# A four-layer network in fourteen stages: the semaphores of a stage are cleared together, mostly in front of the next stage's work on GpSimd

## The reference, cut to what matters

```python
xn = _layernorm(x, axis=-1)
s = _L0_attn_ref(xn, ...)          # layer 0: an RWKV-like recurrence over time
g = _silu(_L0_ffn_ref(xn, ...))    # layer 0: 48 experts, each takes the tokens that score highest
x = x + s * g
...                                # layers 1 to 3 in the same form
return x
```

## The kernel before, in words

| Stage function | Rounds behind it | Semaphores cleared |
|---|---|---|
| `open_phase` | 4 | 26 |
| `rwkv_pre_phase` | 3 | 101 (4, 1, 96) |
| `scan_and_experts_phase` | 6 | 156 (1, 108, 8, 17, 6, 16) |
| `rwkv_close_phase` | 4 | 32 |
| `split_and_choose_phase` | 6 | 50 |
| `attention_and_experts_phase` | 7 | 71 |
| `close_and_split_phase` | 4 | 42 |
| `maxima_and_mlp_phase` | 9 | 50 |
| `causal_phase` | 3 | 20 |
| `inertia_phase` | 1 | 22 |
| `norm_and_split_phase` | 3 | 30 |
| `column_attention_phase` | 3 | 14 |
| `l2_gelu_and_rows_phase` | 2 | 24 |
| `ssm_phase` | 3 | 86 (52, 2, 32) |
| together | 58 | 724 |

## Time and profile before

### The profile page before, as it was taken

One profiled execution on the slowest core, in us unless ns is written; L12 is line 12 of the kernel. 1 busy time (PEld: TensorE's weight loads), 2 busy tenths in 40 slices (PEclk: granted clock), 3 DMA queues, 4 the chain that ended last, 5 costly groups with the idle time before them and its releaser, 6 DMA issues. The chain is left out here.

```text
span 3016.3 us, 37549 instructions
## 1 busy us (share of the span) xinstructions
PE 2424.1 (80%) x10280; PEld 1059.8 (35%) x10280; DVE 2173.8 (72%) x5978; ACT 1702.1 (56%) x3085; POOL 1015.0 (34%) x979
## 2 busy tenths in 40 slices
PE   6665477885869989769999989967778888868887
PEld 2211266662334434333333333323331111224443
DVE  6999589994676665455555646668659999667776
ACT  4454344543646666441211248855569999777775
POOL 0222589981334544140000024400020000038886
PEclk8777567767879999889999999989889999989999
DMA  3112676415456655331011113300031111011110
GB/s 127 56 56 70 154 134 110 89 25 141 136 154 136 118 114 110 110 110 32 27 32 31 28 43 94 84 4 0 0 110 42 44 44 44 22 34 35 38 39 25
DMA packets 295990, 211.39 MB, mean 70 GB/s; under 512 B 155336, under 2 KB 263800, under 8 KB 295160
## 3 DMA queue, kind: packets, MB, share of 16 engines
q1 hardware_dynamic: 257840, 191.80, 24.1%
q0 software_dynamic: 19712, 14.96, 3.8%
q10 hardware_dynamic: 18256, 2.52, 0.5%
HBM read 136.18 MB, written 62.52 MB: 66 GB/s over the span
## 5 line engine op out<-in xcount | busy, mean ns | idle before, releaser
L3125 ACT ACTIVATE ca_pw<-ca_ps,ca_mx 128x512 f32<-128x512 f32 x512 | 342.7, 934 | 9.3 <-DVE ca_mx L3161 9.3
L2999 DVE CUSTOM_DVE_ANT_0 mx_sums<-mx_ps,w_w2f 128x512 f32<-128x512 f32 (+3 forms) x512 | 220.3, 486 | 156.7 <-PE mx_ps L2977 156.7
L3161 DVE TENSOR_REDUCE ca_mx<-ca_ps 128x1 f32<-128x512 f32 x512 | 311.0, 673 | 1.2 <-PE ca_ps L3091 1.2
L2956 PE MATMUL gm_ps<-gm_h,w_w2f 128*128 128x512 f32 x512 | 245.4, 612 | 0.0
L3125 ACT ACTIVATION_READ_ACCUMULATOR ca_pw<-ca_ps,ca_mx 128x1 f32 x512 | 232.0, 453 | 0.0
L3091 PE MATMUL ca_ps<-qs,ks 128*128 128x512 bf16 x512 | 175.7, 395 | 50.3 <-ACT ca_pw L3125 33.4
L2694 ACT ACTIVATE ta_pw<-ta_ps,w_cst 128x1280 f32<-128x1280 f32 x128 | 168.0, 1322 | 44.4 <-PE ta_ps L2574 30.9
L3031 ACT ACTIVATE gm_h<-gm_ps,w_w2f 128x512 f32<-128x512 f32 x64 | 44.0, 688 | 253.1 <-PE gm_ps L2956 253.1
L2420 ACT ACTIVATE at_pw<-at_ps 128x1280 f32<-128x1280 f32 x128 | 154.8, 1236 | 27.6 <-PE at_ps L2385 27.6
L2826 DVE TENSOR_TENSOR ta_pw<-ta_pw,w_cst 128x384 f32<-128x384 f32 x128 | 70.5, 551 | 128.6 <-ACT ta_pw L2694 100.7
L2739 POOL DMA_INDIRECT Acc<-XN,f_idx x64 | 105.5, 1648 | 157.7 <-DVE XN L2797 143.0
(11 more groups left out here) (578 smaller groups left out, 6278.4 us busy)
## 6 DMA issues: line engine op xcount, KB each, us to landing
Pd<-s_p SPq DMA_DIRECT2D x48, 384.0 KB, 2.9
ex_w<-e_w SPq DMA_DIRECT2D x48, 256.0 KB
Qd<-rp_q SPq DMA_DIRECT2D x4, 2048.0 KB, 9.6
ss_ellb<-Rd SPq DMA_DIRECT2D x32, 256.0 KB
qs<-Pd SPq DMA_DIRECT2D x32, 192.0 KB
ks<-Pd SPq DMA_DIRECT2D x32, 192.0 KB
Pd<-cs_p SPq DMA_DIRECT2D x16, 384.0 KB
GX<-Qd SPq DMA_DIRECT2D x44, 128.0 KB
```

The costliest lines, as they stand in the source:

```text
L2956: last = pe.matmul(mps[:, f, :], W(("h1", "h2")[n - 2])[:, j * 512 + f * 128:j * 512 + (f + 1) * 128], src[:, j, :], start=(j == 0), stop= ...
L2999: last = v.tensor_tensor_reduce(out=sums[:, u, at:at + n], in0=ps[:, u, at:at + n], in1=K["w2f"]("down")[:, T - n:T], scale=-1.0, scalar=3 ...
L3125: act.activation(pw[:, h % BUF, jk, :], ps[:, (h * NB + jk) % BANKS, :], ACT.Exp, bias=mx[:, h % H, jk:jk + 1], accum_out=z[:, h % H, jk:j ...
L3161: v.tensor_reduce(mx[:, h % H, jk:jk + 1], ps[:, q % BANKS, :], AX.X, ALU.max, negate=True).then_inc(S["top"], 1)
```

## The change

Semaphores are no longer cleared by each call of `sems`. A new class `Stage` takes the place of `ExitStack` in all fourteen stage functions and collects every semaphore of the stage in one list, `used`. When the stage is left, `retire` is called last. In three stages (`rwkv_pre_phase`, `scan_and_experts_phase` and `ssm_phase`, which are given `at_once=True`) it clears the whole list and adds one barrier. In the other eleven it only keeps the list in `K["spent"]`. The next stage allocates its own semaphores first, which therefore get other numbers, and `stage_block`, which stands where `nc.Block()` stood, then has POOL clear the spent list, with no barrier, directly in front of POOL's branch into that stage. The other engines branch without it. Where the numbers of a list don't lie side by side, the clear becomes several instructions, one for each run of numbers. The function `norm_phase` is removed, which moves every line behind it up by 43 in the changed kernel.

```diff
+class Stage(ExitStack):
+    def __init__(self, nc, K, at_once=False):
+        super().__init__()
+        self.used = []
+        self.callback(retire, nc, K, self.used, at_once)
+
+def retire(nc, K, used, at_once):
+    if at_once:
+        nc.clear_and_free_semaphores(used)
+        nc.all_engine_barrier()
+    else:
+        K["spent"] = used
+
+def stage_block(nc, K, ctx):
+    if K["spent"]:
+        nc.clear_and_free_semaphores(K["spent"])
+        K["spent"] = []
+    return ctx.enter_context(nc.Block())
+
 def sems(nc, ctx, tag, names, lanes=1):
     made = {n: [nc.alloc_semaphore(f"{tag}_{n}{a}") for a in range(lanes)] for n in names.split()}
-    ctx.callback(clear, nc, [s for lane in made.values() for s in lane])
+    ctx.used += [s for lane in made.values() for s in lane]
     return made if lanes > 1 else {n: s[0] for n, s in made.items()}
-
-def clear(nc, used):
-    nc.clear_and_free_semaphores(used)
-    nc.all_engine_barrier()
-
-def norm_phase(nc, K, layer, src="X", dst="XN", gain=None, shift=None):
...
@@ rwkv_pre_phase, scan_and_experts_phase, ssm_phase @@
-    with ExitStack() as ctx:
+    with Stage(nc, K, at_once=True) as ctx:
...
-        block = ctx.enter_context(nc.Block())
+        block = stage_block(nc, K, ctx)
@@ the eleven other stages @@
-    with ExitStack() as ctx:
+    with Stage(nc, K) as ctx:
...
-        block = ctx.enter_context(nc.Block())
+        block = stage_block(nc, K, ctx)
@@ network @@
-        K = {"A": A}
+        K = {"A": A, "spent": []}
```

More of the change, by code:

```diff
@@ L25, in sems @@
 def sems(nc, ctx, tag, names, lanes=1):
     made = {n: [nc.alloc_semaphore(f"{tag}_{n}{a}") for a in range(lanes)] for n in names.split()}
-    ctx.callback(clear, nc, [s for lane in made.values() for s in lane])
+    ctx.used += [s for lane in made.values() for s in lane]
     return made if lanes > 1 else {n: s[0] for n, s in made.items()}
-def clear(nc, used):
-    nc.clear_and_free_semaphores(used)
-    nc.all_engine_barrier()
-def norm_phase(nc, K, layer, src="X", dst="XN", gain=None, shift=None):
-    X, XN, cst = K[src], K[dst], K["cst"]
-    L = 4
-    with ExitStack() as ctx:
[L44 to L47, removed]
-        block = ctx.enter_context(nc.Block())
[L50 to L87, removed]
-                n = i * L
-                for a in range(L):
-                    act.wait_ge(S["cent"][a], i + 1)
-                    act.wait_ge(S["xn"][a], i)
-                    act.activation(sq[:, a, :], xc[:, a, :], ACT.Square).then_inc(S["sq"][a], 1)
-                for a in range(L):
-                    act.wait_ge(S["var"][a], i + 1)
-                    act.activation(sq[:, a, :], ps[:, L + a, :], ACT.Ln,
-                                   bias=cst("eps")).then_inc(S["std"][a], 1)
-                for a in range(L):
-                    act.wait_ge(S["std"][a], i + 1)
-                    act.activation(sq[:, a, :], sq[:, a, :], ACT.Exp, scale=-0.5).then_inc(S["rstd"][a], 1)
```

30 lines of the change are left out of this document (14 added, 16 removed).

## The result

The changed kernel takes 2988.12 us (median of four runs, 2984.46 to 2992.42), the kernel before 3019.23 (3019.06 to 3020.13): a ratio of 0.9899 [0.9887, 0.9911]. That is 31.1 us less, where 23.0 were predicted. The profiled execution took 2987.44 us, and its span is 2985.2, 31.1 less than the span in the earlier trace rows.

What follows compares the result with a forecast made beforehand. No engine bounds the whole; stretches between stages where nobody works lie on the path. Removing 27.5 us less 4.1 added gives 23.4, less 0.43 at the causal stage 23.0: from 3019.1 to 2996.1 us, range 2989 to 3002.

Steps and rivals of the forecast that it cites:

- What a round costs, and what is removed: Between stages: 58 rounds of POOL's drain, clear and a barrier, 0.376 us each plus the clear, 27.5 us removed.
- What is added: Behind the three stages that clear at once: 1.07, 1.44 and 1.6 us come back, together 4.1 us.
- the smaller signs: Causal stage: PE's first matmul within 0.4 us of the release, POOL's memset some 0.7 us behind PE's start.
- The causal stage: At its start POOL's deferred clears delay SP's loads, and PE waits 0.43 us longer; bounds 0 and 0.68.
- The claim that all other starts hide their clear: Outside the causal stage, POOL's late first work or later waits hide deferred clears of 0.3 to 0.5 us.
- I centre on zero and leave 5 us on either side: Inside stages: PE's clock may shift either way, so no net term, with 5 us allowed each way.
- those of before within 2 us or so each: All stages: their lengths between their ends should stay as before, within 2 us or so each.
- More gain: Stage starts: shorter stands keep PE's clock high at three or four starts, 5 us more go, around 2991; chance 0.10.
- The branch has to be paid: Thirteen stage starts: without rounds each waits for instruction fetches, 33.5 us lost, about 3029; slower has chance 0.02.
- Less gain: Stage starts: every deferred clear delays its stage, 5 us rather than 0.43 come back, around 3000.7 and above; chance 0.12.
- The change doesn't do what it says: Stage ends: a long list's clear costs as much as its parts and rounds, time stays 3019; no change has chance 0.03.

Runs made afterwards that it cites:

- e3: Changed kernel with every stage clearing its one list at once plus one barrier, nothing deferred: 3001.6 us, 0.995.
- e4: Changed kernel with 55 barriers that clear nothing behind the first stage: 3014.2 us, 0.9991.
- e7: Changed kernel with 20 barriers that clear nothing in front of `rwkv_pre_phase`: 3008.6 us, 0.9962.
- e8: Kernel before with all 58 clears, but only one barrier per stage, behind its last clear: 3010.6 us, 0.9963.
- e12: Changed kernel with the maxima stage clearing its semaphores at once, with one barrier: 2990.8 us, 0.9908.
- e11: Changed kernel with POOL, in the causal stage alone, clearing the spent semaphores behind its first two memsets: 2993.8 us, 0.9917.
- e15: Changed kernel with 14 barriers that clear nothing behind the first stage, on a fourth chip: 2998.6 us, 0.9937.
- e5: Changed kernel again, no edit, on a second chip: 2999.0 us, 0.9929.
- e2: Changed kernel again, no edit, on a first chip: 2989.2 us, 0.9903.
- e1: Kernel before again, no edit, on a first chip: 3018.2 us, 0.9998.
- e10: Kernel before again, no edit, on a third chip: 3017.3 us, 0.9998.
- e9: Changed kernel again, no edit, on a third chip: 2991.3 us, 0.9906.
- e13: Changed kernel again, no edit, on a fourth chip: 2989.9 us, 0.9912.

## Why the prediction was right in its mechanism and wrong in its number

**What a round costs, and what is removed: right.** 27.5 us predicted, 27.5 measured. (The price was read from one stage end; the measured sum is over all fourteen.) The price of 0.376 + 0.031 us + 5.4 ns for each semaphore held. e3, e4, e7 and e8 take different parts of it away, and the time went along.

**What is added: right.** 4.1 predicted, 4.11 measured, each of the three within 0.05 us. Of the smaller signs, PE's first matmul of the causal stage stands 0.12 us behind the release in four traces of the changed kernel (0.50 in the first comparison, where the record of the first matmul is missing), and POOL's memset stands 0.6 us behind that matmul, not 0.7.

**The causal stage: right in its start, a little small in its sum.** 0.43 us predicted; SP's load is 0.37 later, PE goes on about 0.5 later. The whole stage, though, is 196.0 to 196.8 us in five traces of the changed kernel and 194.6 to 195.3 in three of before, 1.4 more on average. e12 brings it back to 194.6, but e11, with the same start of the chain, only to 195.8; e3 (196.2) and e8 (198.8) have that start too, and e15 has a deferred clear and takes 195.3. So the length doesn't follow the clear. It goes with PE's clock (no run sets the clock alone, so this is read from the traces and not tested). These are the 12.3 us behind the release in the kernel before and in e12, then in the changed kernel, e11 and e8:

```profile
1777.41:1789.71 12.30, 9.51 (x45) 3.42 (x45) 6.77 (x10) 8.84 (x8) 9.05 (x13) 0.70 0.56 105
1756.93:1769.23 12.30, 9.98 (x45) 3.39 (x46) 6.77 (x10) 9.06 (x8) 9.05 (x13) 0.68 0.64 102
```
```profile
1752.38:1764.68 12.30, 8.70 (x32) 3.13 (x33) 6.67 (x10) 8.38 (x7) 8.82 (x13) 0.50 0.61 96
1755.79:1768.09 12.30, 10.00 (x36) 3.49 (x37) 6.66 (x10) 8.38 (x7) 8.71 (x13) 0.51 0.63 101
1766.44:1778.74 12.30, 9.61 (x34) 3.27 (x35) 6.77 (x10) 8.38 (x7) 9.04 (x13) 0.50 0.64 102
```

At a granted clock of 0.70 PE has done 45 matmuls in them, at 0.50 it has done 32 to 36; e5 and e2 lie between, at 0.58 and 0.64. Over the whole stage the lower level lasts 10.3 to 11.0 us in the three traces of before and 13.3 to 15.9 in the five of the changed kernel. Why it lasts longer there is open; e11 and e8 show that the deferred clear is not needed for it.

The claim that all other starts hide their clear held for the starts, but its cover was read too wide. The 98.1 and 25.6 us of the earlier trace rows reach back into the stages ahead; counted from the release, POOL's first work in `rwkv_pre_phase` comes at 53.3 us and in the attention stage at 7.8, both still far more than the clears take.

There is one more stage that grew, `column_attention_phase` (354.6 to 354.9 before, 356.0 to 356.3 in every trace of the changed kernel), but at its end: the last 32 matmuls have a median of 839 ns instead of 592, and the granted clock over the last 13.3 us is 0.86 instead of 0.91. It is so in every kernel that is made from the changed one (356.0 to 356.4), e3 among them, in which nothing is deferred, and not in e8 (355.2); so this isn't the deferred clear either. The rows are those of the kernel before and of the changed one, each over the last 10 to 12 us of the stage:

```profile
L3102 PE MATMUL ca_o<-ca_pw,ca_vs x32: 592/592/617, 2604.5 to 2607.5; 128*32 128x512 f32 x32
```
```profile
L3059 PE MATMUL ca_o<-ca_pw,ca_vs x32: 592/839/1061, 2573.6 to 2578.3; 128*32 128x512 f32 x32
```

**The step that failed: "I centre on zero and leave 5 us on either side", and with it that the lengths of the stages would be "those of before within 2 us or so each".** It put all that can differ inside the stages down to PE's clock, and bounded it by three or four starts. In the first comparison the stages together differed by 7.7 us and the attention stage alone by 7.5. Of this 3.7 us are two stops, which stand in the one trace and not in the other and come in either kernel (e5 against e1 and e10), and up to 3.8 are PE's clock in that stage. The step rightly expected the clock to go either way, but sized it from the starts alone, and it had no term for stops. The other stages that moved did so with the clock as well. From before to the changed kernel the maxima stage went from 446.6 to 444.1 us, and PE's time at its lower level in it from 31.3 to 27.7 us; the inertia stage from 227.5 to 225.1, and that time from 50.2 to 44.4; `rwkv_pre_phase` from 287.7 to 289.7, and that time from 137.6 to 149.1.

The range had no room for scatter either: the three runs of before spread by 1 us, while executions of the one kernel on one chip scatter by 2 to 3.5 us (3010 to 3022 in e9's and e10's company). That scatter goes with PE's clock too: among the 9 to 21 executions of before on each chip the time falls by 0.9 to 1.5 us for each 0.001 of mean granted clock. A difference of two medians of four runs has at least 1.5 us of scatter, and a row of one trace against another far more. That the time fell outside the range at all was in part bad luck: the medians of the four repeats, 2989.2, 2999.0, 2991.3 and 2989.9, all lie inside it.

**How much of the 31.1 us is the change.** On four chips, with before beside it, the changed kernel gained 27.7, 22.2, 27.9 and 26.7 us by the means, 26.1 together. Its standard error is near 0.7 from the scatter of the executions, and 1.3 from that of the four gains among themselves. The forecast of 23.0 is 3 too low by that, and the first comparison's 31.1 is 5 high; at two to three standard errors both are likely to be more than scatter, and neither is certain. The traces don't place the 3 us: the fourteen stages sum to 2985.1 us in three traces of before and to 2984.6 in five of the changed kernel, and single stages moved both ways (norm and split in layer 2 -1.4, column attention +1.4, causal +1.4). By those sums the change is worth 23.9, but single traces differ so much (2979 to 2989 us before, 2980 to 2991 in the changed kernel) that this has a standard error of 3.5 us, and 26.1 is within it. Whether 2 to 3 us come on top of the rounds is open.

**The rivals.** "More gain" named PE's clock, and a gain by it isn't shown, though the mean granted clock rose from 0.890 to 0.892 in e2, e5, e9 and e13's company. What went had a low clock itself, as the kernel before shows in three stretches between stages:

```profile
43.60:45.00 1.40, 0.00 (x0) 0.00 (x0) 0.00 (x0) 0.00 (x0) 0.00 (x0) 0.65 0.00 0
696.50:699.00 2.50, 0.00 (x0) 0.00 (x0) 0.00 (x0) 0.00 (x0) 0.00 (x0) 0.50 0.00 0
333.00:334.80 1.80, 0.00 (x0) 0.00 (x0) 0.00 (x0) 0.00 (x0) 0.00 (x0) 0.50 0.00 0
```

Taking 23.4 us at some 0.58 (the mean of these three and of the earlier trace rows) out of 3016 at 0.890 lifts the mean by 23.4 x 0.31 / 2993 = 0.0024 with no matmul faster. The start of the causal stage did not get the faster clock that this rival hoped for, although the stand of all engines ahead of it is 1.52 us instead of 5.5; over the first 12.3 us it got a slower one, 0.50 against 0.70 in the rows above. The stand is this:

```profile
1750.94:1752.46 1.52, 0.00 (x0) 0.00 (x0) 0.00 (x1) 0.00 (x1) 0.00 (x0) 0.54 0.09 22
```

"The branch has to be paid" is refuted: ACT's first instruction of the causal stage stands 0.08 us behind the release, SP's first of `column_attention_phase` likewise (2228.15 behind 2228.07), with no rounds ahead of either. By the Trainium skill, Runtime: NRT & Kernel Launch, Instruction fetch mechanics, a taken branch stalls unless its target is already fetched; no start here shows that stall, and whether the targets had been fetched beforehand no run tells. "Less gain" is refuted for the starts other than the causal one. "The change doesn't do what it says" is refuted by the 22 clears and 3 barriers and by the 4.11 us.

## What to carry to other kernels

Time in which no engine works came back about one for one here, whatever filled it, so price it from the sequencer's own rows and not from busy shares; the price was right to 0.1 us. A sum made from rows is no sharper than the run it is compared with: before giving a range, allow for the scatter of executions (2 to 3.5 us of 3000 here) and for waits that one trace has and the next of the same kernel hasn't. When two traces differ by more than the change explains, find the stages that hold it, set their lengths beside PE's granted clock in them, and run the old kernel again on the same chip before giving the change the credit.

## What the runs showed of the hardware

- A barrier of all five engines costs 0.328 us when nothing else is waited for (e4); some in a row take 0.6 to 0.8. Behind a clear it adds 0.25 us (e8).
- One clear takes about 31 ns and 5.4 ns for each semaphore, up to 156 of them (0.872 us). POOL's drain ahead of it grows as well, from 66 ns (the median) to 203 ahead of 101 semaphores and 277 ahead of 156.
- DVE, ACT and SP, which wait for results of PE, can stand still for about 2 us behind PE's last matmul and go on within 0.06 us of each other, at fixed places of the program while POOL's gathers are under way: on one chip of four (e5 to e8), and in the first trace of the kernel before. What holds them up is open.
- A stage of the same work is longer or shorter with the time that PE spends at its lower clock level: the causal stage takes 194.6 us with 10.3 us at that level (e10) and 196.8 with 15.9 (e2).
